# Row maxima of a sliding-window attention: 32 x 32 TensorE tiles with 160 keys each, and one VectorE copy and one reduction over four PSUM banks

## The reference

```
h = layernorm(x) * (1 + ca) + sa
# attention: 16 heads of 16 channels, causal, window of 128 keys
band = (j > i) | (i - j > 128)
q, k, v = (ln1(h) @ Wq + bq), (ln1(h) @ Wk + bk), (ln1(h) @ Wv + bv)
attn = softmax(q @ k.T / sqrt(16) + where(band, -inf, 0))
h = h + (attn @ v) @ Wo + bo
h = h + gelu(ln2(h) @ W1 + b1) @ W2 + b2
x = x + ga * h
h = layernorm(x) * (1 + cb) + sb           # second part
xr, xk = mix of h and h shifted by one token
x = x + gb * sigmoid(xr @ Wr.T) * (relu(xk @ Wk.T)**2 @ Wv.T)
```

## Time and profile before

| | |
|---|---|
| median of three runs | 715.37 us |
| profiled execution | 715.73 us, of which 714.0 us are the span of the core |
| PE busy | 607.8 us (85%), 5110 matmuls |
| DVE busy | 519.3 us (73%), 1362 instructions |
| ACT busy | 470.0 us (66%) |
| POOL busy | 355.5 us (50%) |
| granted TensorE clock, mean over the span | 0.911 |

### The profile page before, as it was taken

How to read it: one execution, slowest core, us unless ns; L and a number is a source line. 1 busy time by engine, 2 the same in 40 slices (tenths; PEclk the granted TensorE clock), 3 DMA queues, 4 the chain that set the end, 5 groups by cost and what they waited for, 6 DMA issues and landing times.

```text
span 714.0 us, 14820 instructions
## 1 busy us (share of the span) xinstructions
PE 607.8 (85%) x5110; PEld 502.6 (70%) x5110; DVE 519.3 (73%) x1362; ACT 470.0 (66%) x808; POOL 355.5 (50%) x512
## 2 busy tenths in 40 slices
PE   5556577778798999989999999999999997989994
PEld 3233466557687887778777877777878876889973
DVE  7574796876798879796989798979896866434332
ACT  2414654668497868786878688868886776773431
POOL 5120525262727483738463855485647455664331
PEclk8656555669999999999999999999999999999997
DMA  3523432131213221322123212331313131101110
GB/s 119 193 63 69 110 81 57 39 97 48 59 44 104 52 67 43 93 73 71 39 67 103 80 34 66 99 90 23 97 26 97 21 91 30 38 2 38 38 37 30
DMA packets 56855, 46.84 MB, mean 66 GB/s; under 512 B 26235, under 2 KB 48061, under 8 KB 56782
## 3 DMA queue, kind: packets, MB, share of 16 engines
q1 hardware_dynamic: 54950, 45.04, 23.8%
q10 hardware_dynamic: 1832, 0.87, 0.4%
HBM read 18.11 MB, written 4.23 MB: 31 GB/s over the span
## 4 chain that ended last, share of the span: by engine, by line
PE 51%; ACT 16%; DVE 12%; issue 11%; POOL 6%; SPq 2%; DMA 1%; POOLq 0%; ACTq 0%; DVEq 0%
PE bank L390 13%; ACT p L689 7%; PE bank L321 4%; DVE bank L1016 3%; PE bank L414 3%; PE bank L266 3%; PE bank L298 3%; PE bank L438 2%; PE bank L426 2%; PE bank L375 2%; DVE nmax L1019 2%; ACT L751 2%; PE bank L377 2%; PE bank L376 2%; PE bank L233 2%
## 5 line engine op out<-in xcount | busy, mean ns | idle before, releaser
L689 ACT ACTIVATE p<-bank,scale_s 128x384 f32<-128x384 f32 (+1 forms) x256 | 121.2, 540 | 49.2 <-PE bank L298 49.0
L1016 DVE COPY_PREDICATED bank<-later,bank 128x254 f32<-128x254 int16 x256 | 95.9, 420 | 56.0 <-PE bank L266 55.8
L390 PE MATMUL bank<-w,hid 128*128 128x256 f32 x512 | 117.6, 383 | 0.1
L1421 POOL TENSOR_SCALAR_AFFINE_SELECT p<-p 128x448 f32<-128x448 f32 x64 | 41.4, 647 | 139.2 <-ACT p L689 138.9
L699 ACT ACTIVATE p_hi<-p 128x1344 f16<-128x1344 f32 x64 | 84.7, 1324 | 36.2 <-POOL p L1426 35.4
L390 PEld LDWEIGHTS bank<-w,hid 128*128 128x128 f32 x512 | 94.9, 190 | 14.6 <-ACT hid L751 1.5
L1434 POOL TENSOR_TENSOR p_lo<-p,p_hi 128x1344 f16<-128x1344 f32 x32 | 87.8, 2743 | 27.3 <-ACT p_hi L699 27.3
L1019 DVE TENSOR_REDUCE nmax<-bank 128x2 f32<-128x258 f32 (+1 forms) x256 | 96.4, 419 | 0.0
L298 PE MATMUL bank<-q_st,k_st 100*128 100x192 f16 (+2 forms) x512 | 66.2, 253 | 21.2 <-DVE qt_lo L990 7.8
L375 PE MATMUL bank<-bt_hi,w_hi 128*128 128x256 f32 x256 | 76.2, 298 | 5.3 <-ACT hid L751 5.3
L377 PE MATMUL bank<-bt_hi,w_lo 128*128 128x256 f32 x256 | 72.2, 282 | 0.0
(11 more groups left out here) (180 smaller groups left out, 1426.7 us busy)
## 6 DMA issues: line engine op xcount, KB each, us to landing
k_st<-kt_hi SPq DMA_DIRECT2D x128, 64.0 KB, 2.0
v_blk<-vn SPq DMA_DIRECT2D x64, 66.0 KB, 2.5
q_st<-qt_hi SPq DMA_DIRECT2D x128, 32.0 KB, 1.9
k_st<-kt_lo SPq DMA_DIRECT2D x64, 64.0 KB, 2.0
x<-x SPq DMA_DIRECT2D x16, 256.0 KB, 3.1
out<-x SPq DMA_DIRECT2D x16, 256.0 KB, 2.4
xa<-x SPq DMA_DIRECT2D x7, 512.0 KB, 3.9
q_st<-qt_lo SPq DMA_DIRECT2D x64, 32.0 KB, 1.9
```

What stands on the lines that cost most here:

```text
L390: last = e.matmul(dst, hid[:, m, t * P:(t + 1) * P], w2[:, m, :], start=(m == 0), stop=(m == MF - 1))
L689: e.activation(p32[gp % 2][:, i * 2 * QW:i * 2 * QW + w], ring_s.at["st", gp, i][:, 0:w], ACT.Exp, scale=scale_s[:, 1:2]).then_inc(s_ex, 1)
L1016: e.copy_predicated(tile(j)[:, own + 1:own + P, :], later[:, :, :].bitcast(I16), allowed).then_inc(s_mov, 1)
```

## The change

The four banks of the ring are now one tensor, `quad`, and one DVE instruction can address all four. On PE, `maxima(u, qt)` no longer multiplies 128 queries by 256 keys but splits the queries into four blocks of 32 (`QB`); each block gets its own 160 keys (`WIN`: the 128 before the block and its own 32), 320 columns, and writes 32 PSUM partitions. That is a 32 x 32 tile of the array per block and pair, 16 matmuls instead of four. For the first 128 queries, where fewer keys exist, key 0 is repeated by a first set of 16 matmuls and the real keys come in a second set. On DVE, one `copy_predicated` of 4 x 62 elements and one `tensor_reduce` of 4 x 258 elements serve all four pairs. All semaphore counts of `mx`, `mxm` and `mov` are a quarter of before. The mask `later` is filled by four `affine_select` instead of one. Besides this, the order of all five lists is written anew.

```diff
-                lo = max(qt - 1, 0) * P
-                w = (qt + 1) * P - lo
-                banks = [ring_s.take(("mx", u, qt, j), s_mx, 16 * u + HQ * qt + j + 1) for j in range(HQ)]
+                for j in range(HQ):
+                    hold(e, *ring_s.take(("mx", u, qt, j), s_mx, 4 * u + qt + 1)[1])
                 e.wait_ge(s_kh, 2 * (u + 1))
-                for bank, free in banks:
-                    hold(e, *free)
-                for j, (bank, free) in enumerate(banks):
-                    rows = slice(2 * HD * j, 2 * HD * (j + 1))
-                    e.matmul(bank[:, 0:2 * w], qt_hi[rows, qt * P:(qt + 1) * P], kt_hi[rows, 2 * lo:2 * (lo + w)],
-                             start=True, stop=True).then_inc(s_mxm, 1)
+                tiles = [(qt * P + qb * QB, quad[qb * QB:(qb + 1) * QB, j, :], slice(2 * HD * j, 2 * HD * (j + 1)))
+                         for qb in range(4) for j in range(HQ)]
+                for q0, dst, rows in tiles:
+                    if q0 < P:
+                        e.matmul(dst[:, 0:2 * (P - q0)].rearrange("p (c a) -> p c a", a=2), qt_hi[rows, q0:q0 + QB],
+                                 kt_hi[rows, 0:2].rearrange("p (o a) -> p o a", o=1).broadcast_to([2 * HD, P - q0, 2]), start=True, stop=True)
+                for q0, dst, rows in tiles:
+                    lo = max(q0 - P, 0)
+                    last = e.matmul(dst[:, 2 * (lo + P - q0):2 * WIN], qt_hi[rows, q0:q0 + QB], kt_hi[rows, 2 * lo:2 * (q0 + QB)],
+                                    start=True, stop=True)
+                last.then_inc(s_mxm, 1)
...
-                for j in range(first, last_):
-                    e.wait_ge(s_mxm, 16 * u + HQ * qt + j + 1)
-                    allowed = tile(j)[:, 0:P - 1, :] if own else tile(j)[:, 0:1, :].broadcast_to([P, P - 1, 2])
-                    e.copy_predicated(tile(j)[:, own + 1:own + P, :], later[:, :, :].bitcast(I16), allowed).then_inc(s_mov, 1)
-                for j in range(first, last_):
-                    e.wait_ge(s_mov, 16 * u + HQ * qt + j + 1)
-                    e.tensor_reduce(nmax[:, :, j, qt], tile(j)[:, max(own - 1, 0):own + P, :].rearrange("p c a -> p a c"),
-                                    AX.X, ALU.max).then_inc(s_mx, 1)
+                e.wait_ge(s_mxm, 4 * u + qt + 1)
+                e.copy_predicated(quad[:, :, 2 * P + 2:2 * WIN], later[:, :].rearrange("p (o c) -> p o c", o=1).broadcast_to([P, HQ, 2 * QB - 2]).bitcast(I16),
+                                  quad[:, :, 0:2 * QB - 2]).then_inc(s_mov, 1)
+                e.wait_ge(s_mov, 4 * u + qt + 1)
+                e.tensor_reduce(nmax[:, :, :, qt].rearrange("p a j -> p j a"),
+                                quad[:, :, 2 * QB - 2:2 * WIN].rearrange("p j (c a) -> p j a c", a=2), AX.X, ALU.max).then_inc(s_mx, 1)
```

More of the change, by code:

```diff
@@ L516, in _ @@
             values(0, 0)
[L517 to L521, removed]
             for b in range(B):
                 u, gp = 2 * b, 8 * b
[L524 to L549, removed]
+                scores(gp - 2, 2, 4)
+                context(gp - 3)
+                maxima(u, 2)
+                transposes_b(u - 3)
+                receptance(u - 5)
+                scores(gp - 1, 0, 2)
+                values(b, 1)
                 keys(u - 5)
                 maxima(u, 3)
-                transposes_b(u - 3)
                 context(gp - 2)
@@ L557, in _ @@
                 values_b(u - 5)
+                scores(gp, 0, 2)
+                up(u - 3, 0, 1)
+                scores(gp, 2, 4)
+                context(gp - 1)
+                maxima(u + 1, 0)
+                up(u - 3, 1, 2)
+                up(u - 3, 2, 3)
+                scores(gp + 1, 0, 2)
+                up(u - 3, 3, 4)
+                transposes_c(u - 1)
+                transposes_d(u - 4)
+                down(u - 3, 0)
+                scores(gp + 1, 2, 4)
+                out_project(u - 2)
+                maxima(u + 1, 1)
+                down(u - 3, 1)
+                if u == 0:
+                    setup_mod_rest()
+                scores(gp + 2, 0, 2)
+                scores(gp + 2, 2, 4)
+                context(gp)
+                maxima(u + 1, 2)
+                keys(u - 4)
+                scores(gp + 3, 0, 2)
+                transposes_a(b + 1)
+                scores(gp + 3, 2, 4)
+                receptance(u - 4)
+                context(gp + 1)
+                maxima(u + 1, 3)
+                transposes_b(u - 2)
+                u, gp = 2 * b + 1, 8 * b + 4
+                context(gp - 2)
+                max_rows(u)
+                project(u + 1)
+                values_b(u - 5)
+                scores(gp, 0, 2)
                 if u == 1:
                     setup_bias()
-                context(gp - 1)
-                scores(gp, 0, 2)
                 scores(gp, 2, 4)
@@ L578, in _ @@
                 down(u - 3, 1)
[L579 to L587, removed]
-                context(gp + 2)
-                scores(gp + 3, 2, 4)
-                values_b(u - 4)
-                max_rows(u + 1)
-                project(u + 2)
-                up(u - 2, 0, 1)
+            scores(NG - 2, 2, 4)
+            scores(NG - 1, 0, 2)
+            receptance(NU - 5)
+            scores(NG - 1, 2, 4)
+            transposes_b(NU - 3)
+            keys(NU - 5)
+            context(NG - 3)
+            up(NU - 3, 0, 1)
+            values_b(NU - 5)
+            context(NG - 2)
             up(NU - 3, 1, 2)
+            up(NU - 3, 2, 3)
             context(NG - 1)
-            up(NU - 3, 2, 3)
+            up(NU - 3, 3, 4)
+            transposes_c(NU - 1)
             transposes_d(NU - 4)
-            transposes_c(NU - 1)
-            up(NU - 3, 3, 4)
             out_project(NU - 2)
             down(NU - 3, 0)
-            out_project(NU - 1)
+            down(NU - 3, 1)
             transposes_b(NU - 2)
-            down(NU - 3, 1)
-            receptance(NU - 4)
             keys(NU - 4)
@@ L850, in _ @@
                 high_p(gp)
[L851 removed]
                 gelu(u - 3, 4, 6)
                 gelu(u - 3, 6, 8)
[L854 to L858 removed]
+                exps(gp + 1, 0, 2)
+                exps(gp + 1, 2, 4)
                 context_t(u - 1)
[L860 removed]
@@ L1003, in rest_v, with maxima @@
                                 parts[:, :, :, HD:2 * HD], ALU.subtract).then_inc(s_v3, 1)
-            def maxima(u, qt, first, last_):
+            def maxima(u, qt):
                 if not 0 <= u < NU:
                     return
-                own = 0 if qt == 0 else P
                 if u == 0 and qt == 0:
```

383 lines of the change are left out of this document (192 added, 191 removed).

## The result

The changed kernel took 725.64 us in the median of four runs (725.04 to 726.03), the kernel before, run beside it, 716.51 (715.28 to 717.93). The ratio is 1.0126, with an interval from 1.01 to 1.0152: slower by 9 us, where 705 and a gain of 11 were forecast. The savings that the forecast counted on came in part; new waits of PE took more than they gave.

A forecast was written before the change was run, and what follows sets the result against it. PE was taken as the bound, DVE close behind. 715.7 + 8 (PE) - 10 (steady waits on DVE) - 4 (fill) - 1 - 4 (start) = 704.7, said as 705; own range 698 to 711, chance 0.40.

The forecast's parts named there:

- the one on DVE's tile: DVE's copies and reductions for a tile of queries: 1.65 us together, 1.35 less, 86 us less busy DVE over 64 tiles.
- Waits on DVE, steady, -10: PE's idle time between 200 and 600 us: 10 of 27 us go as DVE's work shrinks; ends 0 and 20.
- PE, +8: Maxima matmuls on PE, steady part: 0.50 us a tile, 0.69 for `qt` = 0, so +8 us; ends 0 and +16.
- larger gain: Rival: the 16 matmuls pass as the four did, DVE's relief takes 14 us of PE's idle time: 690; chance 0.15.
- DVE's prices: Maxima instructions on DVE: reduction of 4 x 258 near 1.26 us, copy near 0.42, DVE busy near 433 us.
- Fill, -4: 0 to 200 us: a third or so of 19.8 us of waits goes, -8, slower pairs +4; ends -9 and +4.
- Start: Setup before the loop: three moved steps, taken as -1 for the first matmul and -4 for the start of unit 1.
- (b): SP's bias rows ready earlier, stacks some 8 us earlier, `project(1)` late next: -4 for unit 1's start; ends 0 and -8.
- (a): First matmul, which waited for DVE until 6.80: memsets moved behind the second maxima, -1 us; ends -3 and +1.
- Rounds: Rival on PE: a block's loads wait until the block before leaves its row group, 1.27 us a tile: 755; chance 0.13.
- absorbed: Rival on PE: each row group's four blocks take turns, 0.70 us a tile, eating DVE's gain: 714; chance 0.22.
- The new order costs waits: Rival: rewritten lists add waits, as DVE's `shift_x` 1.4 us a batch behind POOL's `rs_x`: 722 to 724; chance 0.10.

The follow-up runs named there:

- the late release alone: The kernel before, with only the four banks of a tile reported free together after its last reduction instead of one by one: 786.84 us against 716.38.

## Why the prediction was wrong

Two of the choices, joint or single release and old or new lists, make four kernels with the same tiles (us, medians):

| | joint release | by bank | joint costs |
|---|---|---|---|
| old lists | 733.75 | 709.76 | 24.0 |
| new lists | 725.64 | 715.42 | 10.2 |
| new lists against old | -8.1 | +5.7 | |

From 716.5 that divides the result: the tiles by bank in the old order give -6.6 against the runs beside them, the joint release takes 24.0, the new lists give back 8.1 of it: +9.3, where +9.1 was measured. (Each number is a difference of medians, good to some 2 us. In the row of the new lists the two kernels differ in the reduction and its release alone. No run has the tiles with four reductions and a joint release, so a share of the long instruction itself is not told apart; the late release alone, on the old maxima, says that the release suffices.) The table of the units, by the same steps, says where: up to unit 6 the three are -5.0, +12.3 and -4.8, from unit 6 to unit 15 they are -1.7, +11.3 and -1.4. So half of the price of the joint release falls in the fill. There the granted clock was lower too: 0.69 over the first 200 us with the joint release in the old lists, 0.76 by bank. Part of this half may be clock; that was not separated. By bank the new lists are worth nothing at unit 6 and cost 7.2 us in the nine units behind it.

Point by point:

- **The failed step** is the one on DVE's tile: "the first two banks came free after 1.5 us, now all four after 1.65. Steps that need one bank gain nothing". Its 1.5 us was a *pair* of copies and a *pair* of reductions, but each reduction reported its own bank: by the earlier trace rows the first was free 302.57 + 0.42 - 301.90 = 1.1 us after DVE began. After, all four take 1.7 us (270.10 to 271.78). So steps that need one bank don't gain nothing; they lose 0.6 us. The numbers for it stood in the earlier trace rows; I counted work where I should have followed one bank. The late release alone (786.84) and the release by bank (-24.0 and -10.2) show that this step decided the sign.
- **It is not the whole miss.** Released by bank, the changed kernel takes 715.42 and not 705: of the 20.6 us between forecast and result the joint release is 10.2. The other 10.4, and 8 more by which PE's own term was too high, lie mainly in the next term, which took DVE's relief for PE's gain. Even the tiles by bank in the old lists gain only 6.6 us.
- **Waits on DVE, steady, -10.** The parts that were named came: 6.3 to 3.2 for the last maxima, 4.9 to 0.2 for `qt_lo`, together 7.8 us. But 8.4 us of waits for one bank are new, and ahead of the maxima matmuls PE waits 19.2, where it was 5.9 before. This second part belongs to the new lists and not to the release: by bank it stays at 19.0 in the new lists and is 9.6 in the old ones. Of the 19.2, 13.3 us are for ACT's exponentials, where it was 5.9: by more than the 5 us that the prediction had named as a sign of being wrong.
- **PE, +8.** Mis-sized: 0.36 us a tile, and for `qt` = 0 both sets together 0.39 (165.83 to 166.22) where 0.69 was taken, so about 0, as the rival "larger gain" had it. (The 0.14 and 0.17 us of latency in the prediction's sums stand in none of its rows.) PE's busy time from 200 to 600 us is 366.8 us, where it was 372.9.
- **DVE's prices.** The reduction 1233 ns (1.26 taken), the copy 419 (0.42). Busy 462.0 where 433 was forecast: a tile's eight instructions overlap at their ends and took 2.7 us (301.90 to 304.64), not 3.0, so a tile saves 1.1 us and not 1.35, 68 us in all; in the old lists it was 65 (454.1 busy), the rest is other DVE work that took longer in the new ones. The waits, not this, decide.
- **Fill, -4.** Wrong in sign: from unit 0 to unit 6 it took 217.7 us, where it was 212.1. The waits for maxima did not fall (27.5 us, 25.5 before, of which the prediction had counted 19.8); released by bank they are 15.5 in the same lists. So it is the same failed step.
- **Start.** (b) was right in size, 4 us, by luck:

```profile
58.00 0.69 ACT L672 ACTIVATE qt_hi<-quad,bias_q 128x512 f16<-128x512 f32 x1 [0.85 <-DMA k_st<-kt_lo]
```

  58.00 against 62.27. But the stack started 3.3 us earlier and not 8, and what ACT waited for last was still the stack's DMA and not `project(1)`, as the prediction had it. By unit 3 nothing is left of it. (a) lost 0.7 us: the first matmul waited 7.5 us for DVE, 6.8 before.
- **The rivals.** "Rounds" and "absorbed" are refuted by 0.36 us. "The new order costs waits" named 722 to 724, nearest to 725.6, and its sign is right where the banks are freed singly (+5.7); but its own place, `shift_x` behind POOL's `rs_x`, is a wait of DVE (6.8 us in 400, up to 1.5 at a time) and none of PE; the wait that costs is ahead of the maxima matmuls. With the joint release the new order helps. No rival named the release.

What stays open: why the new lists with the old maxima cost 33 us and not 5.7 was not followed further than its waits; why two reductions a tile in the old lists are 6 us slower than four; how much of each price goes through the granted clock; and whether the new start is worth the 1 or 2 us that the last pairs show.

## What to carry to other kernels

Before instructions are fused over buffers of a ring, follow the first buffer and not the sum: count from the producer's start to the moment when the first one can be taken again, and look who stands next on the engine that waits. On an engine that isn't the bound, less work that hands over its first result later can make the kernel slower; here a reduction for each bank cost 0.2 us of DVE a tile and was worth 10 to 24 us. Nor is a wait of the bounding engine gone when its cause is made faster: look what would hold it next. An order of work that suits one moment of release can cost time with another.

## What the runs showed of the hardware

- Sixteen matmuls in tiles of 32 x 32, four in each group of 32 rows, took 0.36 us in all, their sixteen loads 0.16. Four matmuls of 512 columns had taken 0.40.
- DVE on PSUM in float32: a maximum over 258, 516 and 1032 elements took 419, 691 and 1233 ns, so some 1.05 ns an element and 150 ns once; a predicated copy of 62 and 248 elements 220 and 419 ns. Fusing four reductions into one saves 0.2 us a tile, since four in a row take 1.43.
- A small DMA behind large ones was slow here. The bias rows' write (2 KB) was issued at 31.34 us, right behind the weight loads, and what reads them back, which waits for it, was issued only at 40.74. The last of the weight loads (768 KB, issued at 30.29) took 10.5 us to land. SP's queue after:

```profile
31.34 0.35 SPq L1681 DMA_DIRECT2D bias_rows<-tr  x1
40.74 0.33 SPq L1683 DMA_DIRECT2D row_b<-bias_rows  x1
```

That is 9.4 us, where the same pair was 1.2 us apart before (40.12, and 41.27). Issued 9 us earlier, the rows were read back 0.5 us earlier. The stack went 3.3 us earlier, and 2.8 of that is because the modulation rows' round trip no longer stood between.
